# The first mixture of the values split around two sums, the gate routed one round sooner, and two rounds of the probabilities turned by TensorE alone

## The chip, the cores and the metric

The kernel runs on one core of one Trainium2 chip. The metric is the device time of one execution in microseconds (us). TensorE (PE) multiplies and transposes, its weight load is listed apart as PEld; VectorE is DVE, ScalarE is ACT, GpSimd is POOL, and SyncE (SP) issues the DMAs.

## The reference

Two blocks with residuals run over x of 8 batches x 512 rows x 512 columns. The first is a cross-attention that the change does not touch. The second, for each batch of T = 512 rows, with H = 8 heads of 64, E = 5 experts and 2 of them picked:

```
wv    = topk_mask(x @ Ws, 2) * sigmoid(x @ Ws)       # per row, head, expert
xv    = einsum('btd,edk->btek', x, Wv)               # five candidate values per row
v     = einsum('bthe,btek->bhtk', wv, xv)            # the mixture: values of each head
probs = softmax((x @ Wq) * scale @ (x @ Wk).T)       # 512 x 512 per head
attn  = probs @ v
out   = einsum('bthe,bthk,ekd->btd', topk_mask(x @ Wd, 2), attn, Wo)
```

The input of this block is layer-normalised, and its output is scaled by tanh of a gate and added to x.

## The kernel before

Every engine has a program of its own, and semaphores tie them together. From about 490 us on the second block runs. For each batch it has 32 tiles of scores (128 rows x 512 keys). A round is four tiles, so a batch has rounds 0 to 7. Two heads share two rounds: even tiles belong to the even head, odd tiles to the odd one. Four banks of PSUM (`ps_s`) hold the tiles of one round.

The loop (`Fori` over B - 1 = 7 passes) is software-pipelined: one pass runs rounds 5 to 7 of batch b, and then rounds 0 to 4 of batch b + 1, with the last work of batch b (rounds numbered 8 to 12) woven in. A part before the loop runs the first batch's rounds 0 to 4, and a part behind it the last rounds. In each round every engine goes through five places in order: SCORES, BEFORE, TURNS, BEHIND, AFTER. The order on each engine is written out by hand in tables (`AT`).

In a round, for the steps that matter here:

- PE makes four score tiles (L2273). VectorE takes each row's maximum (`row_max`, L1880), and ScalarE exponentiates into a probability tile (`scores_exp`, L1701).
- The probabilities must be turned for the product with the values. There are two ways. By TensorE: four 128x128 transposes a tile back into the tile's own `ps_s` bank (`turn_probs`, L2281), and a ScalarE copy to `pt` (`probs_copy`, L1710). Or by VectorE: one block transpose of two tiles (`turn_blocks`, L1886), and four DMAs of 128 KB that SyncE issues (`move_blocks`, L1542). Even tiles always go by VectorE. Odd tiles go by TensorE, but in rounds 4, 6 and 7 (`ALL_BY_VECTOR`) by VectorE too.
- The next round's scores need the banks: they wait for the exponentials or for the copies (`pt_ready`).

The mixture is GpSimd's. `mix_values(b, p)` makes the values of the head pair p with five products (L1610) and four sums (L1616), and `values(b, p)` on PE (L2297) waits for it; for p = 0 that product stands at the end of round 3. The mixture needs `pick`, which VectorE makes on this path: `compare` (L1969), `count_better`, `count_values` (L1985) in round 0's TURNS, and `invert` (L1989) and `route_values` (L1996, L2001) in round 1, behind the four row maxima. GpSimd's other work is `mix_sums`: each adds one head's products (`mix_product`, L1900, on VectorE) into `z` (L1628). At the head of a pass's second half GpSimd adds those of heads 4 and 5 of batch b, whose products VectorE makes in round 1 of the next batch, and starts on the mixture 0 of batch b + 1 behind them.

Of the kernel before, what the change touches and what calls it, by code (L numbers as in the profile page):

```python
# [1167 lines left out]
def expert_attention(nc, block, both, x1, g_ffn, wk, wo, out):  # L1168
# [62 lines left out]
    COEFFICIENTS_AT = (3, 5, 7, 8)  # L1231

    ALL_BY_VECTOR = (4, 6, 7)
    PRODUCTS_AT = (5, 7, 9, 10)
    LAST_SUMS_AT = (10, 11)
    NORMALISE_AT = -3
# [35 lines left out]
    with ExitStack() as mem:  # L1272
# [214 lines left out]


        def heads_moved(r):
            return range(2 if r in ALL_BY_VECTOR else 1)  # L1490

        def tiles_moved(r):

            return sum(2 * len(heads_moved(i)) for i in range(r))

        def odd_tiles(n):

            return sum(m // BANKS not in ALL_BY_VECTOR for m in range(1, n + 1, 2))

        def transfers(r):  # L1500

# [4 lines left out]
            return b * transfers(ROUNDS - 2 + r % 2) + transfers(r + ROUNDS * earlier) - earlier * transfers(  # L1506
                ROUNDS - 2 + r % 2)

        def odd_turned(b, n):
            earlier = n < 0  # L1510
            return b * odd_tiles(STEPS - 1) + odd_tiles(n + STEPS * earlier) - earlier * odd_tiles(STEPS - 1)

        def all_turned(n):

            return (B - 1) * odd_tiles(STEPS - 1) + odd_tiles((CUT + 1) * BANKS - 1) + n + 1 - (CUT + 1) * BANKS

        POOL_SUMS, LAST_PAIR = H - 3, PAIRS - 1


# [67 lines left out]
        @block.gpsimd  # L1587
        def _(pool):
            for k in range(ND):
                take_weight_lo(pool, "wk", k)  # L1590
            first_end(pool)
            pool.memset(beaten[:], 0.0).then_inc(cleared, 1)
            pool.wait_ge(cleared, 1)
            pool.memset(wo2[HALF:P, 1, LAST, :].bitcast(F32), 0.0).then_inc(cleared, 1)

            def mix_values(b, p, first=False):

                count = (b * PAIRS + p) * V_STEPS
                if p == 0:
                    pool.wait_ge(pick_ready, b + 1)  # L1600
                    pool.wait_ge(xv_ready, b * NT + NT)
                    if first:
                        pool.wait_ge(w_lo["wx"], ND)
                if not first:

                    pool.wait_ge(o_ps, b * PAIRS - PAIRS + p + 1)
                acc = v_acc[:, p]
                shape = [P, NT, 2, DH]
                for e in range(E):
                    pool.tensor_tensor(v_tmp[:] if e else acc, xv[:, :, e, :].unsqueeze(2).broadcast_to(shape),  # L1610
                                       pick[:, e, :, 2 * p:2 * p + 2].unsqueeze(3).broadcast_to(shape),
                                       ALU.mult).then_inc(v_steps, 1)

                    pool.wait_ge(v_steps, count + 2 * e + (0 if e else 1))
                    if e:
                        pool.tensor_tensor(acc, acc, v_tmp[:], ALU.add).then_inc(v_steps, 1)  # L1616

                        pool.wait_ge(v_steps, count + 2 * e + 1)

            def mix_sums(b, p):  # L1620

                for h in (2 * p, 2 * p + 1):
                    if h:
                        pool.wait_ge(z_dve, b * H + h + 1)
                        if h >= 2:
                            pool.wait_ge(z_pool, b * POOL_SUMS + h - 1)
                        zv = z.rearrange("p t (e k) -> p t e k", e=E)
                        pool.tensor_tensor(zv, zv, z_tmp[:, h % 2], ALU.add).then_inc(z_pool, 1)  # L1628

            def rest(b, first=False):  # L1630
                for p in range(1, PAIRS):
                    mix_values(b, p, first)
                for p in range(LAST_PAIR - 1):
                    mix_sums(b, p)

            def last_sum(h, tiles, made, added):

                pool.wait_ge(z_dve, (B - 1) * H + h + 1)
                pool.wait_ge(z_last, added)
                if made:  # L1640
                    pool.wait_ge(z_pool, (B - 1) * POOL_SUMS + made)
                pool.tensor_tensor(z_by_expert[:, tiles], z_by_expert[:, tiles], last_product(h)[:, tiles],
                                   ALU.add).then_inc(z_pool, 1)

            mix_values(0, 0, True)
            rest(0, True)
            with pool.Fori(0, B - 2) as b:
                mix_sums(b, LAST_PAIR - 1)
                mix_values(b + 1, 0)
                rest(b + 1)  # L1650
            mix_sums(B - 2, LAST_PAIR - 1)
            for p in range(PAIRS):
                mix_values(B - 1, p)
            everything, second_tiles = slice(0, NT), HALVES[1][1]
            last_sum(3, everything, 0, 2)

            pool.wait_ge(coef_ready, B * PAIRS)
            last_sum(4, everything, 1, 2)

            last_sum(5, second_tiles, 2, 5)  # L1660

        @block.scalar
        def _(act):
# [18 lines left out]
            def place_free(b, n, first):  # L1682

                r = n // BANKS
                if first and r < 2:
                    return
                if n % BANKS == 0:
                    act.wait_ge(moved[r % 2], moved_through(b, r - 2))
                elif n % 2 not in heads_moved((r - 2) % ROUNDS):
                    act.wait_ge(pt_ps, odd_turned(b, n - 2 * BANKS))  # L1690

            def scores_exp(b, n, first):
                act.wait_ge(nmax_ready, b * STEPS + n + 1)
# [9 lines left out]

            def probs_copy(b, n, first):
                h, t = head_tile(n)
                act.wait_ge(pt_ps, odd_turned(b, n))
                if n % BANKS == 1 and (h >= 4 or not first):

                    act.wait_ge(o_ps, b * PAIRS + h // 2 - 1)
                act.activation(turned(n), scored(n), ACT.Copy).then_inc(pt_ready, 1)  # L1710
# [60 lines left out]
            def step(b, n, place, first=False):  # L1771

                if place == SCORES:
                    if n in OUT_AT and not first:
                        out_copy(b, OUT_AT.index(n), first)
                    if n == NORMALISE_AT and not first:
                        normalise(b, (0, 1))
                    if 0 <= n < ROUNDS:
                        for tile in range(n * BANKS, n * BANKS + BANKS):
                            scores_exp(b, tile, first)  # L1780
                    if n in OUT_AT and first:

                        out_copy(b, OUT_AT.index(n), first)
                elif place == BEFORE:
                    units_hi(b, units_at(n, BEFORE, table=FIRST_AT if first else AT), first)
                    if n == 0:

                        act.wait_ge(logits_ready, b * NT + NT)
                        act.activation(sig[:], logits[:, 0], ACT.Exp, scale=-1.0).then_inc(sig_exp, 1)
                elif place == TURNS:  # L1790
                    if n == COPY_LAST_AT:

                        copy_last(b)
                    if 0 <= n < ROUNDS and n not in ALL_BY_VECTOR:
                        for tile in range(n * BANKS + 1, n * BANKS + BANKS, 2):
                            probs_copy(b, tile, first)
                elif place == BEHIND:
                    if n == NORMALISE_AT and not first:
                        normalise(b, (2, 3))
                    units_hi(b, units_at(n, BEHIND, AFTER, table=FIRST_AT if first else AT), first)  # L1800
# [66 lines left out]
        def _(dve):  # L1867
# [136 lines left out]
            def step(b, n, place, first=False):  # L2004

                if place == SCORES:
# [3 lines left out]
                    if 0 <= n < ROUNDS:  # L2010
                        for tile in range(n * BANKS, n * BANKS + BANKS):
                            row_max(b, tile)
                    if n == 1:
                        invert(b)
                        route_values(b, first)
                elif place == BEFORE:
                    if n in PRODUCTS_AT:
                        for h in range(2):
# [6 lines left out]
                elif place == TURNS:  # L2025
# [5 lines left out]
                    if n == 0:  # L2031
# [2 lines left out]
                        compare(b)  # L2034
                        count_better(b)
                        count_values(b)
                elif place == BEHIND:
                    units_lo(b, units_at(n, BEHIND, AFTER, table=FIRST_AT if first else AT), first)

# [116 lines left out]
        def _(pe):  # L2156
# [99 lines left out]
            def scores(b, n, first, freed=None):  # L2256
# [8 lines left out]
                elif n >= BANKS or not first:  # L2265
# [1 line left out]
                    if (n // BANKS - 1) % ROUNDS in ALL_BY_VECTOR:  # L2267
                        pe.wait_ge(p_exp, b * STEPS + n + 2 - BANKS)
                    else:
                        pe.wait_ge(pt_ready, odd_turned(b, n + 1 - BANKS))  # L2270
                for m, (l, r) in enumerate(PASSES):
                    for a in range(2):
                        end = pe.matmul(ps_s[:, (n + a) % BANKS, :], q2[head_rows(a), p % 2, l, t * P:(t + 1) * P],  # L2273
# [10 lines left out]
            def values(b, p, first):  # L2284

                if not {2 * p, 2 * p + 1} <= set(ALL_BY_VECTOR):
                    pe.wait_ge(pt_ready, odd_turned(b, PAIR * p + PAIR - 1))
                for r in (2 * p, 2 * p + 1):
                    pe.wait_ge(moved[r % 2], moved_through(b, r))
                pe.wait_ge(v_steps, (b * PAIRS + p + 1) * V_STEPS)  # L2290
                if p or not first:
# [9 lines left out]
            def step(b, n, place, first=False, last=False):  # L2301

                if 0 <= n < ROUNDS:
                    if place == SCORES:
                        for pair in range(n * BANKS, n * BANKS + BANKS, 2):
                            scores(b, pair, first)
                    elif place == TURNS and n not in ALL_BY_VECTOR:
                        for tile in range(n * BANKS + 1, n * BANKS + BANKS, 2):
                            turn_probs(b, tile)
                for what in units_at(n, place, table=FIRST_AT if first else AT):  # L2310
                    shared(b, *what, first, last)
# [175 lines left out]
```

## Time and profile before

| what | us |
|---|---|
| median of 3 runs | 1139.66 (1139.25 to 1140.40) |
| the profiled execution's own time | 1140.54 |
| its span in the trace | 1138.8 |
| PE busy / DVE / ACT / POOL | 1103.0 / 926.2 / 568.1 / 657.9 |
| POOL products of the mixtures, 160 | 185.2 |
| POOL sums within the mixtures, 128 | 165.8 |
| row maxima, DVE | 158.6 |

Busy time is the union of an engine's instructions as the profiler records them. The ends of PE's matmuls are modelled, so for PE the distance from one start to the next says more than a duration. Idle time is listed with the instruction that came after it and the one that released it. A line of the timeline merges instructions of one kind that follow on each other, with their number behind an x.

### The profile page before, as it was taken

How to read it: one execution, taken by the hardware profiler on the slowest of the kernel's cores; microseconds unless marked ns; L12 is line 12 of the kernel's file. 1: busy time of each engine (PE TensorE's matmuls, PEld its weight loads, DVE VectorE, ACT ScalarE, POOL GpSimd, SP SyncE). 2: the span in 40 equal slices, each digit the busy share in tenths (PEclk: the TensorE clock that was granted, in tenths of full speed). 3: DMA queues.
4: the chain of work that ended last, by engine and by line, in shares of the span. 5: the costliest groups of instructions: out<-in, count | busy, mean ns of one | idle time of the engine just before them, and what ended most of it. 6: DMA issues, size and time to landing. Idle time of an engine off the chain costs nothing.

```text
span 1138.8 us, 18705 instructions
## 1 busy us (share of the span) xinstructions
PE 1103.0 (97%) x5709; PEld 836.8 (73%) x5709; DVE 926.2 (81%) x1609; ACT 568.1 (50%) x1295; POOL 657.9 (58%) x476
## 2 busy tenths in 40 slices
PE   7999999999999999999999999999999999999988
PEld 6888888888888888886676766767667666767655
DVE  7988787878777775768798797887988987988986
ACT  7634444444444443436556555455556555555533
POOL 2645252525243433328849669489398497595793
PEclk9999999999999999999999999999999999999999
DMA  5441414141414122343333524424326235244241
GB/s 204 148 139 47 130 56 129 55 129 55 129 55 129 55 92 93 131 130 83 103 76 110 166 55 147 129 55 150 108 59 199 74 94 161 77 116 121 53 134 38
DMA packets 89277, 119.97 MB, mean 105 GB/s; under 512 B 9120, under 2 KB 52896, under 8 KB 89248
## 3 DMA queue, kind: packets, MB, share of 16 engines
q1 hardware_dynamic: 89248, 119.61, 35.1%
q8 instruction: 15, 0.25, 0.1%
q14 instruction: 14, 0.11, 0.0%
HBM read 58.76 MB, written 16.78 MB: 66 GB/s over the span
## 4 chain that ended last, share of the span: by engine, by line
PE 68%; POOL 13%; DVE 9%; issue 5%; ACT 4%; POOLq 0%; DMA 0%; DVEq 0%; ACTq 0%
PE ps_f L992 23%; PE ps_s L992 8%; PE ps_o L2297 7%; PE ps_h L992 7%; POOL spare L1610 6%; PE ps_r L2219 6%; POOL spare L1616 5%; PE ps_r L2252 5%; PE ps_s L2273 4%; PE ps_r L2228 3%; DVE nmax L1880 2%; DVE beaten L1969 1%; POOL z L1628 1%; ACT tmp L1701 1%; ACT probs_odd L1701 1%
## 5 line engine op out<-in xcount | busy, mean ns | idle before, releaser
L1610 POOL TENSOR_TENSOR spare<-xv,pick 128x512 f32<-128x512 f32 x160 | 185.2, 1157 | 35.2 <-DVE pick L1996 22.3
L1880 DVE TENSOR_REDUCE nmax<-ps_s 128x1 f32<-128x512 f32 x256 | 158.6, 681 | 55.0 <-PE ps_s L2273 54.0
L1628 POOL TENSOR_TENSOR z<-z,z_tmp 128x1280 f32<-128x1280 f32 x35 | 102.7, 2934 | 123.5 <-DVE z_tmp L1900 121.0
L1616 POOL TENSOR_TENSOR spare<-spare 128x512 f32<-128x512 f32 x128 | 165.8, 1295 | 10.0
L1701 ACT ACTIVATE tmp<-ps_s,nmax 128x512 f32<-128x512 f32 x124 | 85.5, 689 | 109.5 <-DVE nmax L1880 109.5
L2297 PE MATMUL ps_o<-pt,spare 128*64 128x512 f32 x496 | 115.7, 609 | 9.2 <-POOL spare L1616 5.1
L254 POOL TENSOR_TENSOR e_t<-e_t 128x512 fp32r<-128x512 f32 x28 | 35.4, 1297 | 135.6 <-ACT e_t L510 135.6
L2273 PE MATMUL ps_s<-k,q 64*128 64x512 f32 x768 | 106.3, 408 | 0.7 <-ACT pt L1710 0.7
L2273 PEld LDWEIGHTS ps_s<-k,q 64*128 64x128 f32 x768 | 67.3, 184 | 47.3 <-issue 34.3
L254 POOL TENSOR_TENSOR c<-stage,c 128x512 fp32r<-128x512 f32 x28 | 41.5, 1514 | 95.8 <-ACT c L250 95.8
L2219 PE MATMUL ps_r<-es_t,c_t 128*128 128x512 f32 x384 | 96.3, 399 | 0.0
L2219 PE MATMUL ps_r<-es_t,wk 128*128 128x512 f32 x384 | 95.0, 396 | 0.0
L992 PE MATMUL ps_s<-c_t,es_t 128*128 128x512 f32 x384 | 92.7, 393 | 2.3 <-DVE es_t L727 2.3
L992 PE MATMUL ps_f<-wec,e_t 128*128 128x512 f32 x384 | 92.1, 392 | 0.0
L992 PE MATMUL ps_f<-weh,eh_t 128*128 128x512 f32 x384 | 91.9, 391 | 0.0
L992 PE MATMUL ps_f<-wh,h_t 128*128 128x512 f32 x384 | 91.3, 389 | 0.5 <-DVE h_t L887 0.5
L992 PE MATMUL ps_h<-es_t,c 128*128 128x512 f32 x384 | 88.7, 390 | 0.2 <-DVE es_t L781 0.2
L2297 PEld LDWEIGHTS ps_o<-pt,spare 128*64 128x64 f32 x496 | 33.6, 139 | 71.3 <-issue 64.5
L992 PEld LDWEIGHTS ps_s<-c_t,es_t 128*128 128x128 f32 x384 | 71.0, 188 | 17.7 <-DVE es_t L727 2.8
L992 PEld LDWEIGHTS ps_f<-wh,h_t 128*128 128x128 f32 x384 | 72.0, 188 | 15.9 <-DVE h_t L887 1.0
L992 PEld LDWEIGHTS ps_h<-es_t,c 128*128 128x128 f32 x384 | 71.9, 188 | 15.1 <-DVE es_t L781 0.3
L992 PEld LDWEIGHTS ps_f<-wec,e_t 128*128 128x128 f32 x384 | 71.4, 188 | 15.0 <-DVE wec L254 0.4
(253 smaller groups left out, 2279.1 us busy)
## 6 DMA issues: line engine op xcount, KB each, us to landing
pt<-tmp SPq DMA_DIRECT2D x248, 128.0 KB, 2.6
stage<-in_x SPq DMA_DIRECT2D x32, 256.0 KB, 3.1
x_sb<-in_x SPq DMA_DIRECT2D x8, 1024.0 KB, 5.3
x_dram<-x_sb SPq DMA_DIRECT2D x32, 256.0 KB, 3.2
stage<-x_dram SPq DMA_DIRECT2D x8, 1024.0 KB, 5.5
x_sb<-x_dram SPq DMA_DIRECT2D x8, 1024.0 KB, 5.6
out_dram<-x_sb SPq DMA_DIRECT2D x31, 256.0 KB, 2.7
pt<-probs_odd SPq DMA_DIRECT2D x60, 128.0 KB, 2.7
```

The source lines that it names most:

```text
L254: return eng.tensor_tensor(pair[:, 1, k, :], operand[:, k, :], pair[:, 0, k, :].bitcast(F32), ALU.subtract)
L992: last = pe.matmul(out, left(l, k), right(r, k), start=start and n == 1, stop=stop and n == ND * len(PASSES))
L1610: pool.tensor_tensor(v_tmp[:] if e else acc, xv[:, :, e, :].unsqueeze(2).broadcast_to(shape), pick[:, e, :, 2 * p:2 * p + 2].unsqueeze(3). ...
L1616: pool.tensor_tensor(acc, acc, v_tmp[:], ALU.add).then_inc(v_steps, 1)
L1628: pool.tensor_tensor(zv, zv, z_tmp[:, h % 2], ALU.add).then_inc(z_pool, 1)
L1701: act.activation(out, scores, ACT.Exp, bias=nmax[:, n:n + 1], accum_out=den[:, h, t:t + 1]).then_inc(p_exp, 1)
L1880: dve.tensor_reduce(nmax[:, n:n + 1], ps_s[:, n % BANKS, :], AX_X, ALU.max, negate=True).then_inc(nmax_ready, 1)
L2219: end = pe.matmul(ps, w2[:, l, k, n * P:(n + 1) * P], y_t2[:, r, k, :], start=m == 0, stop=m == len(every) - 1)
L2228: end = pe.matmul(ps[:, 0:NX], y_t2[:, l, k, n * P:(n + 1) * P], wx2[:, r, k, :], start=m == 0, stop=m == len(every) - 1)
L2252: end = pe.matmul(ps, z_t2[:, zt(l, k), n * P:(n + 1) * P], wo2[:, r, k, :], start=m == 0, stop=m == len(every) - 1)
L2273: end = pe.matmul(ps_s[:, (n + a) % BANKS, :], q2[head_rows(a), p % 2, l, t * P:(t + 1) * P], k2[head_rows(a), p % 2, r, :], start=m == 0, ...
L2297: end = pe.matmul(ps_o[head_rows(a), :], v_acc[:, p, k, a, :], rows, start=k == 0, stop=k == NT - 1)
```

## The change

It has three parts.

1. `NONE_BY_VECTOR = (0, 2)`: in rounds 0 and 2 of each batch all four tiles are turned by TensorE and copied by ScalarE. VectorE's block transpose of the even tiles and its four DMAs are gone there. The waits are counted anew: `tensor_turned` counts tiles instead of odd tiles, the copies wait for the place in `pt` at the round's first tile, and the product with the values doesn't wait for DMAs of such rounds.
2. VectorE's `invert` and `route_values` move from round 1, behind its four row maxima, to round 0, directly behind `count_values`.
3. GpSimd makes the first two experts' part of mixture 0 (two products and a sum) ahead of the sums of heads 4 and 5, and the other three experts' part behind them (`turn_of`).

```diff
+    NONE_BY_VECTOR = (0, 2)
         def heads_moved(r):
-            return range(2 if r in ALL_BY_VECTOR else 1)
+            return () if r in NONE_BY_VECTOR else (0, 1) if r in ALL_BY_VECTOR else (0,)
+        def tensor_tiles(r):
+            return [n for n in range(r * BANKS, r * BANKS + BANKS) if n % 2 not in heads_moved(r)]
...
+        EARLY = 2
...
+            def turn_of(b):
+
+                mix_values(b + 1, 0, experts=range(EARLY))
+                mix_sums(b, LAST_PAIR - 1)
+                mix_values(b + 1, 0, experts=range(EARLY, E))
+
             with pool.Fori(0, B - 2) as b:
-                mix_sums(b, LAST_PAIR - 1)
-                mix_values(b + 1, 0)
+                turn_of(b)
                 rest(b + 1)
...
-                    if n == 1:
-                        invert(b)
-                        route_values(b, first)
...
                         count_values(b)
+                        invert(b)
+                        route_values(b, first)
...
-                        pe.wait_ge(pt_ready, odd_turned(b, n + 1 - BANKS))
+                        pe.wait_ge(pt_ready, tensor_turned(b, n + 1 - BANKS))
...
-                    elif place == TURNS and n not in ALL_BY_VECTOR:
-                        for tile in range(n * BANKS + 1, n * BANKS + BANKS, 2):
+                    elif place == TURNS:
+                        for tile in tensor_tiles(n):
                             turn_probs(b, tile)
```

## Rows read from the trace of the kernel before

**Rows 1.** The page: busy time by engine, and the chain that ended last.

```profile
PE 1103.0 (97%) x5709; PEld 836.8 (73%) x5709; DVE 926.2 (81%) x1609; ACT 568.1 (50%) x1295; POOL 657.9 (58%) x476
...
PE 68%; POOL 13%; DVE 9%; issue 5%; ACT 4%; POOLq 0%; DMA 0%; DVEq 0%; ACTq 0%
```

**Rows 2.** Busy time in a window as long as one loop pass.

```profile
core 0: us, PE busy (x) PEld busy (x) DVE busy (x) ACT busy (x) POOL busy (x), PEclk, DMA share, GB/s
609.30:688.48 79.18, 76.74 (x422) 53.60 (x421) 67.95 (x97) 43.12 (x109) 58.46 (x42) 1.00 0.40 113
```

**Rows 3.** PE's waits in such a window: total, times, longest.

```profile
PE ps_r L2228 <- DVE es_t L1934: 1.0, 1, 1.0
PE ps_o L2297 <- POOL spare L1616: 0.7, 1, 0.7
PE ps_r L2242 <- DVE z L1911: 0.2, 1, 0.2
PE ps_s L2281 <- ACT probs_odd L1701: 0.2, 1, 0.2
PE ps_s L2281 <- ACT spare L1701: 0.2, 1, 0.2
```

**Rows 4.** Timeline of PE, rounds 0 to 3 of a pass: start, duration, work.

```profile
731.39 0.60 PE L2281 MATMUL ps_s<-ident,probs_odd 128*128 128x128 f32 x4
732.18 0.66 PE L2281 MATMUL ps_s<-ident,probs_odd 128*128 128x128 f32 x4 [0.20 <-ACT probs_odd L1701]
...
740.39 1.03 PE L2281 MATMUL ps_s<-ident,spare 128*128 128x128 f32 x8
...
749.78 1.04 PE L2281 MATMUL ps_s<-ident,probs_odd 128*128 128x128 f32 x8
750.58 2.98 PE L2219 MATMUL ps_r<-es_t,wk 128*128 128x512 f32 x12
...
761.89 3.65 PE L2297 MATMUL ps_o<-pt,spare 128*64 128x512 f32 x16 [0.73 <-POOL spare L1616]
```

**Rows 5.** Timeline of DVE, rounds 0 and 1 of the same pass.

```profile
731.56 1.25 DVE L1886 STREAM_TRANSPOSE tmp<-tmp 128x1024 f32<-128x1024 f32 x1 [0.41 <-ACT tmp L1701]
732.73 1.93 DVE L1969 TENSOR_TENSOR beaten<-logits 128x256 bf16<-128x256 f32 x8
...
736.18 0.24 DVE L1985 TENSOR_SCALAR sig<-sig 128x160 f32<-128x160 f32 x1
...
736.93 2.48 DVE L1880 TENSOR_REDUCE nmax<-ps_s 128x1 f32<-128x512 f32 x4
739.32 1.14 DVE L1989 RECIPROCAL sig<-sig 128x160 f32<-128x160 f32 x1
...
740.99 2.88 DVE L1900 TENSOR_TENSOR z_tmp<-ps_r,coef 128x1280 f32<-128x1280 f32 x2
```

**Rows 6.** Timeline of ACT, rounds 0 and 1 of the same pass.

```profile
732.01 0.24 ACT L1751 ACTIVATE logits<-ps_r 128x80 f32<-128x80 f32 x1
...
732.67 1.11 ACT L1710 ACTIVATE pt<-ps_s 128x512 f32<-128x512 f32 x2
...
740.30 0.21 ACT L1701 ACTIVATION_READ_ACCUMULATOR spare<-ps_s,nmax 128x1 f32 x1
```

**Rows 7.** Timeline of POOL, the last sum of mixture 0, same pass.

```profile
760.56 1.28 POOL L1616 TENSOR_TENSOR spare<-spare 128x512 f32<-128x512 f32 x1
```

**Rows 8.** Timelines of PE and POOL in the first batch.

```profile
513.45 1.25 PE L2281 MATMUL ps_s<-ident,spare 128*128 128x128 f32 x8
...
521.83 1.18 PE L2281 MATMUL ps_s<-ident,probs_odd 128*128 128x128 f32 x8
...
559.47 0.63 PE L2234 MATMUL ps_r<-ident,spare 128*128 128x128 f32 x4 [1.26 <-ACT logits L1751]
...
514.46 2.18 POOL L1610 TENSOR_TENSOR spare<-xv,pick 128x512 f32<-128x512 f32 x2 [22.28 <-DVE pick L1996]
```

**Rows 9.** Windows with PEclk behind an idle stretch and over 16 transposes.

```profile
1106.00:1108.00 2.00, 1.00 (x4) 0.45 (x6) 2.00 (x2) 0.00 (x0) 1.92 (x2) 0.50 0.13 45
1119.20:1121.40 2.20, 2.20 (x20) 1.95 (x18) 2.17 (x4) 2.02 (x7) 1.13 (x1) 1.00 0.00 0
```

More of the change, by code:

```diff
@@ L1489, in heads_moved, with tiles_turned @@
         def heads_moved(r):
-            return range(2 if r in ALL_BY_VECTOR else 1)
+            return () if r in NONE_BY_VECTOR else (0, 1) if r in ALL_BY_VECTOR else (0,)
         def tiles_moved(r):
             return sum(2 * len(heads_moved(i)) for i in range(r))
-        def odd_tiles(n):
-            return sum(m // BANKS not in ALL_BY_VECTOR for m in range(1, n + 1, 2))
+        def tensor_tiles(r):
+            return [n for n in range(r * BANKS, r * BANKS + BANKS) if n % 2 not in heads_moved(r)]
+        def tiles_turned(n):
+            return sum(m in tensor_tiles(m // BANKS) for m in range(n + 1))
         def transfers(r):
@@ L1507, in moved_through, with tensor_turned @@
                 ROUNDS - 2 + r % 2)
-        def odd_turned(b, n):
+        def tensor_turned(b, n):
             earlier = n < 0
-            return b * odd_tiles(STEPS - 1) + odd_tiles(n + STEPS * earlier) - earlier * odd_tiles(STEPS - 1)
+            return b * tiles_turned(STEPS - 1) + tiles_turned(n + STEPS * earlier) - earlier * tiles_turned(STEPS - 1)
         def all_turned(n):
-            return (B - 1) * odd_tiles(STEPS - 1) + odd_tiles((CUT + 1) * BANKS - 1) + n + 1 - (CUT + 1) * BANKS
+            return (B - 1) * tiles_turned(STEPS - 1) + tiles_turned((CUT + 1) * BANKS - 1) + n + 1 - (CUT + 1) * BANKS
+        EARLY = 2
         POOL_SUMS, LAST_PAIR = H - 3, PAIRS - 1
@@ L1594, in _, with mix_values @@
             pool.memset(wo2[HALF:P, 1, LAST, :].bitcast(F32), 0.0).then_inc(cleared, 1)
-            def mix_values(b, p, first=False):
+            def mix_values(b, p, first=False, experts=range(E)):
                 count = (b * PAIRS + p) * V_STEPS
-                if p == 0:
+                if p == 0 and 0 in experts:
                     pool.wait_ge(pick_ready, b + 1)
@@ L1603, in mix_values @@
                         pool.wait_ge(w_lo["wx"], ND)
-                if not first:
+                if not first and 0 in experts:
                     pool.wait_ge(o_ps, b * PAIRS - PAIRS + p + 1)
@@ L1608, in mix_values @@
                 shape = [P, NT, 2, DH]
-                for e in range(E):
+                for e in experts:
                     pool.tensor_tensor(v_tmp[:] if e else acc, xv[:, :, e, :].unsqueeze(2).broadcast_to(shape),
@@ L1647, in _ @@
             with pool.Fori(0, B - 2) as b:
-                mix_sums(b, LAST_PAIR - 1)
-                mix_values(b + 1, 0)
+                turn_of(b)
                 rest(b + 1)
-            mix_sums(B - 2, LAST_PAIR - 1)
-            for p in range(PAIRS):
+            turn_of(B - 2)
+            for p in range(1, PAIRS):
                 mix_values(B - 1, p)
@@ L1686, in place_free @@
                     return
-                if n % BANKS == 0:
+                before = (r - 2) % ROUNDS
+                if n % BANKS == 0 and heads_moved(before):
                     act.wait_ge(moved[r % 2], moved_through(b, r - 2))
-                elif n % 2 not in heads_moved((r - 2) % ROUNDS):
-                    act.wait_ge(pt_ps, odd_turned(b, n - 2 * BANKS))
+                if n % 2 not in heads_moved(before):
+                    act.wait_ge(pt_ps, tensor_turned(b, n - 2 * BANKS))
             def scores_exp(b, n, first):
@@ L1705, in probs_copy @@
                 h, t = head_tile(n)
-                act.wait_ge(pt_ps, odd_turned(b, n))
-                if n % BANKS == 1 and (h >= 4 or not first):
+                act.wait_ge(pt_ps, tensor_turned(b, n))
+                if n == tensor_tiles(n // BANKS)[0] and (h >= 4 or not first):
                     act.wait_ge(o_ps, b * PAIRS + h // 2 - 1)
@@ L1793, in step @@
                         copy_last(b)
-                    if 0 <= n < ROUNDS and n not in ALL_BY_VECTOR:
-                        for tile in range(n * BANKS + 1, n * BANKS + BANKS, 2):
+                    if 0 <= n < ROUNDS:
+                        for tile in tensor_tiles(n):
                             probs_copy(b, tile, first)
@@ L2286, in values @@
                 if not {2 * p, 2 * p + 1} <= set(ALL_BY_VECTOR):
-                    pe.wait_ge(pt_ready, odd_turned(b, PAIR * p + PAIR - 1))
+                    pe.wait_ge(pt_ready, tensor_turned(b, PAIR * p + PAIR - 1))
                 for r in (2 * p, 2 * p + 1):
+                    if not heads_moved(r):
+                        continue
                     pe.wait_ge(moved[r % 2], moved_through(b, r))
@@ L2306, in step @@
                             scores(b, pair, first)
-                    elif place == TURNS and n not in ALL_BY_VECTOR:
-                        for tile in range(n * BANKS + 1, n * BANKS + BANKS, 2):
+                    elif place == TURNS:
+                        for tile in tensor_tiles(n):
                             turn_probs(b, tile)
```

## The prediction

> **What bounds the kernel now.** I read the page first: PE is busy 97% of the span, no other engine above 81% [rows 1]. The chain that ended last says 68% PE and 13% POOL, so something makes PE wait for GpSimd. The windows by loop pass tell how much that is. A pass takes 79.18 us, and PE is busy for 76.74 of them [rows 2]; five windows of that length, one after the other, hold the same busy time to 0.03 us. So in a pass 2.44 us are idle, and the list of PE's waits names 2.3 of them: 1.0 for the layer norm's operand (`es_t`), 0.7 for GpSimd's first mixture, and three of 0.2 for z and for exponentials [rows 3]. The reader is to see two things here. The loop runs at the pace of PE's own queue, with a handful of short waits in it. And POOL's 13% of the chain is misleading: the chain walks back through GpSimd's whole mixture because PE waits for its last instruction, but the wait is 0.73 us a pass [rows 4], and that alone can be won there. Hence the account below: PE's added work, less the waits that go, plus the waits that come.
>
> **PE's added work.** In rounds 0 and 2 two more tiles of four transposes each: 16 transposes a pass. Their price is the distance of starts, since durations overlap: eight at 749.78, the next work at 750.58, so 0.80 us for eight and 0.40 a tile [rows 4]. That is 1.60 us a pass.
> A page of the Trainium skill ("TensorE: Matmul & The Clock Gate", Part 4) gives about 275 ns for one transpose in a kernel's context. The rows have eight within 1.04 us, so here that is no engine time of its own; by 275 ns each the pass would grow by 4.4 us for this part instead of 1.6.
>
> Round 0: PE has turned tile 1 at 731.39 and then waits for the exponential of tile 3, which it gets at 732.18 [rows 4]. With four tiles, 0, 1 and 2 fill the time from 731.39 to 732.59 and tile 3 follows without a wait, ending at 732.99 and not at 732.58. So here two tiles cost 0.40, not 0.80. Round 2: the eight transposes run without a wait, so the full 0.80 is paid.
>
> ScalarE gets four copies more a pass, of about 0.55 us (1.11 for two [rows 6]). In round 0 the four run from 732.67 to about 734.9; the next scores start some 3 us behind the last transpose, as a product for q or k stands between (2.98 us at 750.58 [rows 4]). They are hidden, and so is the longer hold of the PSUM banks. Without that cover, 1.1 us a round would show, and in round 2 of the first batch it does in part: there no product stands between, but the pace of copies overlaps with that of the transposes, and I take the 0.80 of the two tiles alone.
>
> VectorE loses one block transpose of 1.25 us [rows 5] in each of the two rounds, and SP eight DMAs a batch. In round 0 little comes of it: `compare` needs the last `logits`, which ScalarE copies behind the exponentials, until 732.25 [rows 6]. It starts at 732.73 now [rows 5] and could start at 732.32. Won: 0.41 us. In round 2 it helps the maxima of round 3 a little, which wait for k's high part anyway. I give it 0.3 us off the two waits of 0.2 for the exponential and for z in round 3 (bounds 0 and 0.4). The removed DMAs hold nobody: the product with the values waits last for POOL.
>
> **The route moved ahead.** `invert` and `route_values` take 1.67 us (739.32 to 740.99 [rows 5]). They now stand ahead of q's low part and the four maxima of round 1. So `count_values` ends at 736.42 - 0.41 = 736.01, the route at about 737.7, and the maxima start at 738.32 instead of 736.93, with q's low part of 0.6 in between: 1.39 us later. They were not waiting for PE at 736.93; VectorE was late already. What queues behind them: ScalarE's four exponentials of round 1, now done at 740.51 [rows 6] + 1.39 = 741.90. PE wants tile 7 at 740.39 + 0.41 + 0.40 (from round 0) = 741.20. New wait: 0.70 us. Bounds: 0 if VectorE keeps up after all; 1.39 if no slack absorbs it. I take 0.70, since both ends of it are starts in one pass. VectorE's products of heads 4 and 5 come 0.3 us sooner than before, as 1.67 has left their place and 1.39 has come: GpSimd isn't later.
>
> **The mixture split.** `pick` is ready near 737.4, GpSimd is idle then, and makes two products and a sum in 3.5 us before the first product of z arrives at 742.3. Mixture 0 then ends some 3.5 us sooner than 761.84 [rows 7], while PE comes to it later than 761.16 (761.89 less the wait). The whole 0.73 us goes, with several us to spare. In the other mixtures GpSimd was ahead already.
>
> **Sum.** A pass: round 0 +0.40, round 1 +0.70, round 2 +0.80, round 3 -0.30, mixture -0.73: +0.87 us. Seven passes: +6.1 us. First batch, ahead of the loop: the shift at the end of round 1's turns is 1.39 (turns start at 513.45 [rows 8], 0.5 of it from round 0, where the exponentials also hold PE), round 2 adds 0.80. Against it, POOL starts on `pick` at 514.46 [rows 8] and will start 3.2 us sooner, which clears the wait of 1.26 us at 559.47, where ScalarE held the logits for the end of the mixtures. Net +0.9 us. The end of the kernel is untouched, and the mixtures have slack there. Total +7.0 us: 1147.5 against the profiled execution's own 1140.54 (span 1138.8), and 1146.7 against the median, which lies 0.88 below it.
>
> **Rivals.**
> *The route costs nothing (15%).* If the maxima of round 1 keep their pace, the 0.70 stays away: a pass costs +0.17, the first batch about nothing: +1.2 us, 1140.9. For it: the exponentials are only 0.3 us ahead of PE's need today, and a small slack elsewhere would decide. Against: every instruction in between starts when the one before ends.
> *Faster (9%): VectorE was the hidden brake.* The largest wait, 1.0 us for `es_t`, runs over maxima, exponentials and VectorE's low part. If 2.5 us less work on VectorE cleared this and every other wait, a pass would change by 1.60 - 2.44 = -0.84 and the whole by -5.9, +0.3 for the first batch: 1134.1. It decides from the point where more than 1.6 us of waits a pass go. Against: the wait lies in round 6, and no work is taken off there; the rows name at most 1.3 us of waits in reach, and 0.2 of them is in round 0's price already.
> *Slower still (12%): no slack.* If the 1.39 us reaches PE in full, that is 0.69 more a pass: +4.8, 1151.5. If ScalarE's copies show as well, up to 1.1 us a round, more. Against: the copies have 3 us of cover.
> *The clock falls (2%).* It stood at 0.50, which is 1.2 GHz, behind PE's idle stretch near the end, but at 1.00 (2.4 GHz) over 16 transposes in a row [rows 9]. Were a stretch as long as a value product (3.65 us [rows 4]) run at the lower level each pass, that would be +3.65 a pass, 1172.
> The same page and part of the Trainium skill says that transposes don't count as work for the clock as matmuls do, which speaks for this rival; the row with 16 of them does not show it.
> *As forecast: 62%.*
>
> **Numbers.** A change within 0.2% (2.3 us) can't be told from none here. Slower: the forecast, the slower still and the clock, 76%. Same: 15%. Faster: 9%. The range runs from the free route, 1140.7, to the full delay, 1151.5; what is outside is most of the faster case, part of the free route and the far end of the slow ones. The forecast's own range, with round 3's gain from 0 to 0.4 and the new wait within 0.3 of 0.70, is 1144 to 1150.
>
> **What would show it.** Right: a window of a pass of about 80.05 us with PE busy near 78.3; no wait of L2297 for L1616; a new wait of some 0.7 us of L2281 for an exponential in round 1; round 0's turns with no wait; maxima of round 1 that start only behind the route. The first batch without the wait at L2234. Wrong: a pass at or under 79.2 us; no wait in round 1; an `es_t` wait that shrank; a new wait of L2273 for L1710, which would be the copies; a clock under 1.00 inside the loop.

## The result and the profile after

The changed kernel takes 1151.26 us (median of 4 runs, 1150.14 to 1154.86), the kernel before 1140.03 in runs beside it: a ratio of 1.0103, 95% interval 1.0087 to 1.012. That is 11.2 us slower. The forecast was slower by 7.0 us. The time lies at the upper edge of the range (1151.5), and outside the forecast's own range of 1144 to 1150.

The page of the changed kernel answers to [rows 1]. PE is still at 97%, with 128 instructions and 12.3 us more of work, and POOL is gone from the chain:

```profile
PE 1115.3 (97%) x5837; PEld 850.7 (74%) x5837; DVE 909.5 (79%) x1593; ACT 583.6 (51%) x1327; POOL 657.1 (57%) x476
...
PE 84%; DVE 7%; ACT 5%; issue 3%; DMA 0%; DVEq 0%; ACTq 0%
```

A loop pass, measured from the first product with Wo (`ps_r<-wo,z_t`, the result product) to that of the next pass, takes 80.67 us and not 79.18. Its window answers to [rows 2]:

```profile
core 0: us, PE busy (x) PEld busy (x) DVE busy (x) ACT busy (x) POOL busy (x), PEclk, DMA share, GB/s
694.68:775.36 80.68, 78.39 (x438) 55.41 (x437) 65.81 (x94) 45.05 (x112) 58.44 (x42) 1.00 0.34 98
```

PE's busy time grew by 1.65 us a pass, as 16 transposes at 0.10 would have it. The idle time should have shrunk, and it is 2.29 us, nearly the old 2.44. So the waits that went were replaced. PE's waits in that window, against [rows 3] (`es_t` is the layer norm's operand):

```profile
PE ps_r L2239 <- DVE es_t L1946: 1.0, 1, 1.0
PE ps_r L2253 <- DVE z L1923: 0.7, 1, 0.7
PE ps_s L2292 <- ACT spare L1713: 0.5, 1, 0.5
```

The wait for GpSimd's mixture is gone. The one for an exponential (0.5) and the one for z (0.7, before 0.2) have taken its place. PE's timeline of the same rounds, against [rows 4]:

```profile
734.79 0.60 PE L2292 MATMUL ps_s<-ident,tmp 128*128 128x128 f32 x4
...
736.10 0.60 PE L2292 MATMUL ps_s<-ident,probs_odd 128*128 128x128 f32 x4
...
744.25 0.60 PE L2292 MATMUL ps_s<-ident,spare 128*128 128x128 f32 x4
745.36 0.66 PE L2292 MATMUL ps_s<-ident,spare 128*128 128x128 f32 x4 [0.51 <-ACT spare L1713]
...
754.36 0.60 PE L2292 MATMUL ps_s<-ident,tmp 128*128 128x128 f32 x4
...
756.03 2.99 PE L2230 MATMUL ps_r<-es_t,wk 128*128 128x512 f32 x12
...
765.29 1.53 PE L2253 MATMUL ps_r<-ident,z 128*128 128x128 f32 x12 [0.71 <-DVE z L1923]
766.75 3.65 PE L2310 MATMUL ps_o<-pt,spare 128*64 128x512 f32 x16
```

Read it by the distance of each start to its partner in [rows 4]. The turns of round 0 start 3.40 us later than there (734.79 to 731.39), those of round 1 3.86, those of round 2 4.58, the product behind round 2's turns 5.45, and the value product at the end of round 3 4.86. The differences are the price of each stretch: round 0 +0.46, round 1 +0.72, round 2 +0.87, round 3 with the mixture -0.59. That is +1.46 of the pass's +1.50. Seven passes give +10.5; the first batch gives +0.5 (559.95 for 559.47 at the transposes of [rows 8]), and the rest of the 11.3 us of the profiled execution (1151.82) lies behind the loop.

VectorE in rounds 0 and 1, against [rows 5]:

```profile
735.68 1.97 DVE L1981 TENSOR_TENSOR beaten<-logits 128x256 bf16<-128x256 f32 x8 [1.13 <-ACT logits L1763]
...
739.44 1.15 DVE L2001 RECIPROCAL sig<-sig 128x160 f32<-128x160 f32 x1
...
741.12 0.68 DVE L1950 SCALAR_TENSOR_TENSOR q<-ps_r,q 128x512 fp32r<-128x512 f32 x1
741.73 2.48 DVE L1892 TENSOR_REDUCE nmax<-ps_s 128x1 f32<-128x512 f32 x4
```

With round 0 laid over round 0 (3.40 off), the maxima of round 1 start at 738.33 on the time scale of [rows 5], where the prediction had 738.32. What it did not have is the z sum at the end of round 3. First the kernel before, VectorE's last z sum with the GpSimd instructions around it and the PE work that waits for it:

```profile
757.50 2.07 DVE L1911 TENSOR_TENSOR z<-z,z_tmp 128x1280 f32<-128x1280 f32 x1
...
756.93 1.29 POOL L1616 TENSOR_TENSOR spare<-spare 128x512 f32<-128x512 f32 x1
758.30 2.18 POOL L1610 TENSOR_TENSOR spare<-xv,pick 128x512 f32<-128x512 f32 x1
...
759.62 1.53 PE L2242 MATMUL ps_r<-ident,z 128*128 128x128 f32 x12 [0.25 <-DVE z L1911]
```

And the changed kernel:

```profile
762.69 2.55 DVE L1923 TENSOR_TENSOR z<-z,z_tmp 128x1280 f32<-128x1280 f32 x1
...
762.60 1.29 POOL L1622 TENSOR_TENSOR spare<-spare 128x512 f32<-128x512 f32 x1
763.97 2.18 POOL L1616 TENSOR_TENSOR spare<-xv,pick 128x512 f32<-128x512 f32 x1
```

The same sum takes 2.07 us in the one and 2.55 in the other. In both it ends about 1.35 us behind the end of the GpSimd instruction that was in progress when it started (758.22 to 759.57, 763.89 to 765.24), and GpSimd's next product takes 2.18 us instead of 1.05. It looks like a lock: the one that comes second stands still until the first is done. The GpSimd sum that the changed kernel's z sum meets belongs to mixture 1: mixture 0 now ends at 760.18, which is 5.1 us sooner against round 0 than before (the prediction had 3.5), and GpSimd goes straight on.

### The profile page after: what moved, and what is told of

It reads as the page before. It is cut to its first block, busy times and chain, and to the rows that moved or that the text cites. A ratio compares the mean times of both kernels' runs of the same rounds, so it can differ in the third digit from the quotient of the medians.

```text
span 1150.0 us, 18942 instructions
## 1 busy us (share of the span) xinstructions
PE 1115.3 (97%) x5837; PEld 850.7 (74%) x5837; DVE 909.5 (79%) x1593; ACT 583.6 (51%) x1327; POOL 657.1 (57%) x476
## 4 chain that ended last, share of the span: by engine, by line
PE 84%; DVE 7%; ACT 5%; issue 3%; DMA 0%; DVEq 0%; ACTq 0%
PE ps_f L992 23%; PE ps_r L2230 11%; PE ps_o L2310 10%; PE ps_s L992 8%; PE ps_s L2284 7%; PE ps_h L992 7%; PE ps_r L2239 5%; PE ps_r L2263 5%; PE ps_s L2292 3%; DVE nmax L1892 3%; PE ps_r L2245 2%; DVE z L1923 2%; ACT tmp L1713 1%; ACT probs_odd L1713 1%; PE ps_r L2253 1%
```

## The experiments

All diffs are against the changed kernel unless said otherwise. A pass is the distance between the first result products of two passes, given as the usual one of a run: but for the last pass here and there, they agree to 0.06 us where nothing else is said.

**Part 1 alone** (rounds 0 and 2 by TensorE).

```diff
-                mix_values(b + 1, 0, experts=range(EARLY))
                 mix_sums(b, LAST_PAIR - 1)
-                mix_values(b + 1, 0, experts=range(EARLY, E))
+                mix_values(b + 1, 0)
```

and `invert` and `route_values` back in round 1, behind the row maxima.

> Part 1 alone: rounds 0 and 2 turned by TensorE, gate's route and mixture as before. Theory of PE's account: round 0 costs 0.46 and round 2 0.86 us a pass, and as PE comes 1.3 us later to the mixture, the wait of 0.73 for GpSimd goes: a pass of about 79.8 us, the whole 4 to 6 us over before. Rival, that part 1 carries all of the loss (copies, banks): 9 us or more over before.

Measured: 1145.20 us, ratio 1.0032 (1.0019 to 1.0045), a pass of 79.67 us. PE still waits 0.6 us for the mixture, since the sums before it come late as well; the wait for z and the waits for exponentials in rounds 0 and 3 are gone. The size is as the account said, its way only partly. By the pass, part 1 carries a third of the loss (0.49 of 1.49 us).

**Parts 1 and 2** (the mixture in one piece): the first diff alone.

> Parts 1 and 2, the mixture in one piece behind the two sums. Theory of the account: the split is worth nothing here, since PE comes over 1 us after the mixture's end in any case, and only the phase of GpSimd's instructions against VectorE's last z sum shifts, by which the wait for z may be anything from 0.2 to 1.3 us: 7 to 13 us over before. Rival, that the split itself costs (sums of heads 4 and 5 held up by the early part): 2 us or more faster than the changed kernel, with the sums' start on GpSimd earlier by as much. Rival, that the split gains: 5 us slower than the changed kernel, with PE waiting for L1622's like.

Measured: 1151.69 us, ratio 1.0102 (1.0085 to 1.0119). That is within the expected 7 to 13 us over before, and no faster than the changed kernel: the split is worth nothing beside the other two. More telling: the profiled execution took 1147.42, and in it the passes are not alike. Two take 79.73 and 79.77 us, the next four 80.72 to 80.77. From the second of the fast passes and from a slow one, VectorE's last z sum, GpSimd's instruction beside it, and PE's turns of z:

```profile
680.76 1.48 DVE L1922 TENSOR_TENSOR z<-z,z_tmp 128x1280 f32<-128x1280 f32 x1
...
680.74 2.64 POOL L1622 TENSOR_TENSOR spare<-spare 128x512 f32<-128x512 f32 x1
...
682.49 1.47 PE L2252 MATMUL ps_r<-ident,z 128*128 128x128 f32 x12
```

```profile
840.28 2.61 DVE L1922 TENSOR_TENSOR z<-z,z_tmp 128x1280 f32<-128x1280 f32 x1
...
840.25 1.29 POOL L1622 TENSOR_TENSOR spare<-spare 128x512 f32<-128x512 f32 x1
...
842.94 1.53 PE L2252 MATMUL ps_r<-ident,z 128*128 128x128 f32 x12 [0.76 <-DVE z L1922]
```

The recorded starts lie within 0.02 to 0.03 us of each other, GpSimd's ahead both times. In the first VectorE takes its 1.48 us and GpSimd's sum stretches from 1.29 to 2.64; in the second it is the other way round, and PE waits 0.76 us. One kernel, one execution, and a pass is 1.0 us longer by who got through first. At such a distance the recorded starts don't tell who that will be.

**Parts 1 and 3** (the route back in round 1).

```diff
+                    if n == 1:
+                        invert(b)
+                        route_values(b, first)
...
-                        invert(b)
-                        route_values(b, first)
```

> Parts 1 and 3, the route back in round 1 behind the row maxima. Theory: the wait of PE in round 1 for the last exponential (0.5 us as recorded, 0.74 from start to start) is the route's, and goes; but the early part of the mixture now starts some 3.5 us later, ends behind the first product for z, and delays the two sums by about 2 us, whose end VectorE's products of head 7 wait for: between 4 and 7 us over before. Rival, that the wait in round 1 comes from the four turned tiles of round 0: the wait stays and the time is that of the changed kernel.

Measured: 1140.53 us, ratio 1.0003 (0.9993 to 1.0013), a pass of 79.03 us. Both changed waits are gone; the only one left on PE is the old 1.0 for `es_t`. I had expected 4 to 7 us over before, since I gave the late sums a price. They have one (VectorE's product of head 7 stands 1.1 us for GpSimd), but round 3's maxima had room for it. The window shows PE at 77.94 of 79.03:

```profile
688.11:767.14 79.03, 77.94 (x438) 55.43 (x436) 64.93 (x95) 45.00 (x112) 58.79 (x42) 1.00 0.35 100
```

So the whole loss hangs on part 2: with it 80.67 a pass, without it 79.03. But only 0.7 of these 1.64 us are the route's own wait in round 1. The rest is the z sum: without part 2 it starts within 0.03 us of a GpSimd sum, gets through first, and takes 1.48 us. In one pass of this same execution, the last, it starts 0.32 us behind that sum instead, takes 2.32 us, PE waits 0.47 us for it, and the pass is 79.71 and not 79.03.

**Part 3 alone** (`NONE_BY_VECTOR = ()` and the route in round 1).

> Part 3 alone: the mixture split, route in round 1, turning as before. Theory: GpSimd fills the 1.7 us between pick and the first product, the mixture ends 1.7 us sooner and PE's 0.73 us wait goes; but the sums end 1.8 us later, VectorE's product of head 7 waits for them about 0.6 us and with it the maxima of round 3, so that PE's wait there grows by that: pass 78.9 to 79.2 us, 0 to 3 us faster than before. Rival, that GpSimd's mixture is the bound by the chain (13% POOL): 1.7 us a pass, 12 us faster.

Measured: 1143.04 us, ratio 1.0027 (1.0015 to 1.004), a pass of 79.57. This miss is of sign. PE's wait for the mixture goes, but its waits for exponentials in round 3 grow to 0.53 and 0.68, because the maxima come later by what the sums held up; without part 1, VectorE's block transpose stands ahead of them too, and there is no room. Splitting at two experts costs more than it brings.

**Part 2 alone** (`NONE_BY_VECTOR = ()`, the mixture in one piece).

> Part 2 alone, the route ahead of q's low part and the maxima of round 1. Theory: the maxima come 1.67 us later, PE waits about 1.4 us (start to start) for the last exponential of round 1, and by that is behind the mixture, whose wait of 0.73 goes: a pass of 79.8 us, up to 80.7 if the z sum meets a GpSimd instruction, 4 to 10 us over before. Rival, that the route is only dear together with part 1 (the parts without it cost nothing, 1140.5 us): a pass of 79.2.

Measured: 1143.25 us, ratio 1.0031 (1.002 to 1.0042), a pass of 79.76. PE's waits in round 1 are 0.52 and 0.68 us, and the mixture's 0.73 is gone. The pass is as expected, at the low end, since the z sum takes 2.08 us here as in the kernel before; the time, 3.6 us over before, is just short of the 4 to 10 expected.

**GpSimd held back for the z sum.** The changed kernel with one wait more:

```diff
                 mix_values(b + 1, 0, experts=range(EARLY, E))
+                pool.wait_ge(z_ready, b * 2 + 2)
```

> The changed kernel with one wait more: GpSimd starts mixture 1 only when VectorE has made the last z sum of the batch before (z_ready). Theory: that sum takes 2.55 us instead of about 1.45 because it stands still while a GpSimd instruction on SBUF is in progress, and PE waits 0.71 us for it; with GpSimd idle the sum takes 1.45 and the wait is gone: a pass of 79.95 instead of 80.67 us, 1146 us, at a GpSimd 4 us later than before. Rival, that the sum is late because the row maxima before it are: its duration may fall, but the wait stays over 0.4 us and the pass at 80.4 or more. Rival, that GpSimd has no slack: PE waits for mixtures 1 to 3.

Measured: 1143.94 us, ratio 1.0036 (1.0022 to 1.005), a pass of 79.73. One wait that lets an engine idle for 4.14 us makes the kernel 7 us faster. VectorE, GpSimd and PE at the end of round 3:

```profile
760.41 1.48 DVE L1924 TENSOR_TENSOR z<-z,z_tmp 128x1280 f32<-128x1280 f32 x1
...
762.05 2.18 POOL L1616 TENSOR_TENSOR spare<-xv,pick 128x512 f32<-128x512 f32 x2 [4.14 <-DVE z L1924]
...
762.14 1.47 PE L2254 MATMUL ps_r<-ident,z 128*128 128x128 f32 x12
```

The z sum is at 1.48 us, and PE turns z without a wait. The wait in round 1 stays as it was (0.52). Nothing waits for mixtures 1 to 3. The pass fell by 0.94, more than the 0.71 of the recorded wait: from the start of round 3's turns to the start of z's it is 1.89 us in the changed kernel (763.40 to 765.29) and 1.02 here (761.12 to 762.14), which is 0.87 of it.

**Only the first product ahead of the sums**, on the kernel before (`EARLY = 1`, `NONE_BY_VECTOR = ()`, the route in round 1).

> The kernel before with only the first product of mixture 0 (1.05 us) ahead of the two sums, instead of two products and a sum. Theory: it fits between pick at 740.9 and VectorE's product at 742.5, so the sums and VectorE's product of head 7 are not held up, and the mixture ends 1.1 us sooner: PE's wait of 0.73 goes and nothing else moves: a pass of 78.45 to 78.7 us, 4 to 5 us faster than before, 1135. Rival, that PE would wait as long for something else (z, exponentials of round 3): within 1 us of before.

Measured: 1134.02 us, ratio 0.9946 (0.993 to 0.9963), a pass of 78.37. The wait for the mixture is gone and every other wait is as it was in [rows 3]. This beats both kernels, by 5.6 and 17 us.

**The same with GpSimd held at mixture 1.**

> As the run with the first product alone ahead, and GpSimd held at mixture 1 until the last z sum is made. Theory of the lock: the wait for z (0.25) goes too, a pass of 78.2 us, 1133. If mixture 1 starts behind the z sum already, as mixture 0 ends late here, nothing changes against that run.

Measured: 1134.28 us, ratio 0.9951 (0.9935 to 0.9968), a pass of 78.34. Nothing changes, the second of the expected cases: what stands in the z sum's way here (2.07 us still) is the end of mixture 0, which the wait doesn't move.

**What a turned round costs**, without the mixture's wait to hide it: the first-product kernel with `NONE_BY_VECTOR = (0,)`, and with `(2,)`.

> The kernel with the first product alone ahead of the sums (pass 78.37 us, no wait for the mixture), and of part 1 only round 0 turned by TensorE. Theory: two more tiles cost 0.87 us from start to start, but 0.40 of it covers the time in which PE waited for the last exponential of round 0: a pass of 78.8 us. Rival, that a tile turned by TensorE costs its full time there: 79.2. Rival, that VectorE's free 1.2 us gives the time back later in the pass: 78.4.

> The same with only round 2 turned by TensorE. Theory: 0.87 us more in round 2, and in round 3, where VectorE has no block transpose ahead of the maxima, the waits for an exponential and for z (0.2 each as recorded) shrink by 0.3 to 0.7: a pass of 78.6 to 78.95 us. If the last z sum meets a GpSimd instruction, up to 1.3 us more at once. Rival, that round 2 costs its 0.87 in full: 79.25.

Measured: round 0, 1138.28 us (0.9979, 0.9967 to 0.9991), a pass of 78.77: +0.40. Round 2, 1134.81 us (0.9946, 0.9923 to 0.9968), a pass of 78.40: +0.03, less than I had allowed. In that run the last z sum starts when GpSimd's product has only 0.15 us left, and takes 1.48 to 1.50 us instead of 2.07. PE's waits in round 3, for an exponential and for z, are both gone: from round 3's turns to z's it is 0.93 us instead of 1.70. The 0.87 of round 2 comes back nearly whole.

## Why the prediction was right and wrong

*The bound.* Right. PE's queue set the pace, and the mixture's wait was worth 0.7 us a pass and no more, whatever POOL's share of the chain. Splitting it at one product brought 0.81 a pass, at a cost of nothing.

*The transposes.* Right: 0.46 in round 0 and 0.87 in round 2, for 0.40 and 0.80. The tile in a row of four takes 0.44 us from start to start and not 0.40 (505.41, 505.85, 506.28 and 734.79 to 736.10 in the timeline after). The copies and the banks were hidden in the loop, as said.

*The route.* Right in place and size: the maxima 1.40 us later for 1.39, PE's turns 0.72 later for 0.70.

*Round 3.* This is the step that failed, in size and sign. The prediction gave "0.3 us off the two waits of 0.2 for the exponential and for z in round 3 (bounds 0 and 0.4)". The exponential's wait did go. But z's grew from 0.25 to 0.71, so that round 3 cost 0.22 instead of giving 0.30 (the stretch of -0.59 above, less the 0.81 that the mixture's wait gave from start to start). Over seven passes that is 3.6 of the 4.2 us by which the forecast was short. The tiles added 0.13 us a pass more, of which the mixture gave 0.08 back. What the step missed is the z sum's own duration. The sum starts 0.26 us sooner against PE's work than before (5.19 us later, PE 5.45), as the prediction would have it, but takes 0.48 us longer (2.55 for 2.07), and +0.22 is the difference. In place of the step stands the lock between VectorE's z sum and GpSimd: shown three ways, by the pair of passes in one execution, by the held-back GpSimd, which won 0.94 us a pass, and by round 2 turned alone, where the sum met only the last 0.15 us of a GpSimd instruction and took 1.50 us. Without the lock, round 3 would have given 0.7 us a pass, more than my upper bound.

The trace of the kernel before had what was needed: the sum's duration varied (1.69 to 2.08 us in its loop), and some of GpSimd's products took 2.18 us and not 1.05. I took the durations as fixed costs of their instructions and moved them about, where they are made by what runs beside them too. The bounds of a term that stands on such a duration should have reached from the sum's bare 1.44 to about 2.65 (1.35 behind a GpSimd instruction of 1.3), against the 2.07 that it took: some 0.6 us to either side of -0.3, by this estimate from -0.9 to +0.3. The +0.22 of the changed kernel and the -0.72 with GpSimd held back both lie in there.
The Trainium skill ("SBUF — State Buffer", "Who interferes with whom") states this: a VectorE instruction with two SBUF inputs and a GpSimd instruction that reads SBUF share a port pair, and the one that starts second stands still until the other has ended. The rows agree where the starts are well apart: in the kernel before, VectorE's sum started 0.57 us behind GpSimd's and took 2.07, and GpSimd's product started 0.80 us behind VectorE's sum and took 2.18 for 1.05. Where they are 0.03 us apart or less, who was first can't be read from the recorded starts.

*The first batch.* +0.5 us for +0.9; the wait at the logits went as predicted.

*The rivals.* "The route costs nothing" fell: the wait of round 1 is there in every kernel with part 2 and in none without. "VectorE was the hidden brake" fell too: the wait of 1.0 for `es_t` is the same in all twelve traces. The clock stood at 1.00 in the loop's windows of all of them. "Slower still" named the price (1151.5) but not the cause: of the 1.39 us it let reach PE in full, 0.72 did, so that its number came out is luck.

*Two sums of the prediction.* The bounds that it gives for its own range, 0.3 on the new wait and 0.3 on round 3, add up to 0.6 us a pass, so to 1150.9 at the upper end and not 1150; the measured time lies outside that too. The free route comes to 1140.9, where the range has 1140.7.

*The parts together.* Alone, parts 1, 2 and 3 cost 5.4, 3.6 and 3.2 us on the medians, and 0.49, 0.58 and 0.39 us a pass, the sum of which is near the whole by chance: parts 1 and 3 together cost 0.7. (Part 1's runs lie at 1143.2 and at 1145.2 to 1145.6, and its ratio of 1.0032 stands for 3.6 us.) The likely reading, argued from the waits above: part 1 gives VectorE the room that part 3 takes, and part 2 takes it away again.

Open: why runs of the changed kernel spread by 4.7 us, where those before spread by 1.7 beside them and by 2.8 in the largest set of 17. Passes that flip by 1.0 us, as in the execution above, would explain runs below the profiled one (1151.82), in which every pass takes the longer time, but not the one of 1154.86 above it. Only the profiled executions show their passes.

## What to carry to other kernels

When one engine sets the pace, price a change by its added instructions from start to start, less each wait that ends there, and look at who else runs at the moment of every wait that moves. Do not carry over the duration of a VectorE instruction with two SBUF inputs if GpSimd runs beside it: find its shortest and its longest, and put both into the range. And give an idle engine only what fits its gap: one product of 1.05 us ahead of the sums won 5.6 us, three instructions of 3.5 us (part 3 alone) lost 3.

## What the runs showed that was not expected

VectorE's sum of two SBUF tensors and a GpSimd instruction, with recorded starts 0.02 to 0.03 us apart, took 1.48 and 2.64 us in one pass, and 2.61 and 1.29 in another of the same execution: a difference of 1.0 us a pass that no line of the code decides. And an engine that was made to wait 4.14 us made the kernel 7.3 us faster (1143.94 for 1151.26).
